# GNN message kernel: one sum along the parts' axis in place of four adds, and VectorE's work behind the table in another order

## The reference, cut to what matters

```python
h = jnp.maximum(_layernorm(x, axis=-1), 0.0)
x_i, x_j = h[dst], h[src]
tmp = jnp.concatenate([x_i, x_j, edge_attr], axis=1)
msg = jax.nn.relu(tmp @ W1 + b1) @ W2 + b2
x = x + jax.ops.segment_sum(msg, dst, num_segments=12500)
```

## Time and profile before

| | |
|---|---|
| time, median of 3 runs | 3531.99 us (3527.91 to 3535.4) |
| profiled execution: time | 3524.77 us |
| profiled execution: span of its instructions | 3522.9 us |
| PE busy | 3298.3 us (94%), 21992 matmuls |
| DVE busy | 2710.3 us (77%) |
| POOL busy | 2665.2 us (76%) |
| ACT busy | 1994.9 us (57%) |
| mean granted TensorE clock | 0.966 |

### The profile page before, as it was taken

The page is one execution under the profiler, slowest core; times in us unless marked ns, Lnnn a source line. Parts: engine busy times, 40 slices in busy tenths (PEclk is TensorE's granted clock), DMA queues, the critical chain, the costliest instruction groups (busy, mean ns, idle before and its releaser), DMA issues.

```text
span 3522.9 us, 96768 instructions
## 1 busy us (share of the span) xinstructions
PE 3298.3 (94%) x21992; PEld 2982.0 (85%) x21992; DVE 2710.3 (77%) x7030; ACT 1994.9 (57%) x7413; POOL 2665.2 (76%) x2768
## 2 busy tenths in 40 slices
PE   7699999999999999999999999999999999999998
PEld 6698888888888888888888888888888888888887
DVE  7787788887777777777777777777777777777774
ACT  6466666655555555555555555555555555555553
POOL 7677777777777777777777777777777777777776
PEclk9999999999999999999999999999999999999996
DMA  9543434333333333333333333333333333333434
GB/s 276 119 110 106 108 107 109 105 106 100 103 102 104 101 104 101 103 101 104 102 102 102 100 105 101 105 100 105 100 104 101 105 101 106 99 106 98 106 100 104
DMA packets 286659, 380.48 MB, mean 108 GB/s; under 512 B 90916, under 2 KB 190549, under 8 KB 285542
## 3 DMA queue, kind: packets, MB, share of 16 engines
q0 software_dynamic: 88064, 177.91, 20.4%
q1 hardware_dynamic: 198342, 201.58, 19.6%
q10 hardware_dynamic: 208, 0.49, 0.1%
HBM read 362.58 MB, written 17.04 MB: 108 GB/s over the span
## 4 chain that ended last, share of the span: by engine, by line
PE 31%; POOL 27%; issue 22%; DMA 8%; ACT 6%; DVE 4%; DVEq 1%; SPq 0%; POOLq 0%; ACTq 0%
POOL gath L540 26%; PE ps L1285 13%; DMA gath<-b_table,idx 7%; PE ps L1269 7%; PE ps L1261 6%; ACT work L675 2%; DVE gath L990 2%; PE ps L1308 2%; ACT gath L656 2%; PE ps L1237 1%; PE ps L1316 1%; PE ps L1295 1%; PE ps L1275 1%; ACT work L698 1%; ACT idx L640 0%
## 5 line engine op out<-in xcount | busy, mean ns | idle before, releaser
L540 POOL DMA_INDIRECT gath<-b_table,idx x2688 | 2588.8, 963 | 826.8 <-issue 757.6
L1285 PE MATMUL ps<-h_tab,p_hot 128*128 128x480 f32 (+1 forms) x6768 | 1588.3, 380 | 0.0
L1285 PEld LDWEIGHTS ps<-h_tab,p_hot 128*128 128x128 f32 x6768 | 1247.7, 195 | 80.9
L675 ACT ACTIVATE work<-ps,work 128x80 f32<-128x80 f32 x4136 | 977.8, 331 | 474.3 <-PE ps L1285 467.3
L656 ACT ACTIVATE gath<-gath 128x512 f32<-128x512 f32 (+1 forms) x768 | 443.6, 578 | 923.5 <-DVE gath L990 920.6
L1269 PEld LDWEIGHTS ps<-onehot,gath 128*128 128x128 f32 x5376 | 696.7, 196 | 262.1 <-ACT gath L656 246.5
L1269 PE MATMUL ps<-onehot,gath 128*128 128x48 f32 x5376 | 743.0, 279 | 167.5 <-ACT gath L656 163.6
L1261 PE MATMUL ps<-rhs,lhs 96*128 96x128 f32 x5376 | 804.9, 292 | 35.5 <-DVE lhs L981 35.5
L990 DVE TENSOR_TENSOR gath<-ps,gath 128x512 f32<-128x512 f32 (+1 forms) x768 | 479.6, 624 | 426.2 <-DMA gath<-b_table,idx 397.4
L1261 PEld LDWEIGHTS ps<-rhs,lhs 96*128 96x128 f32 x5376 | 694.4, 200 | 37.2 <-issue 35.7
L981 DVE TENSOR_SCALAR_CACHE_REDUCE lhs<-nodes 48x512 f32<-48x512 f32 (+1 forms) x768 | 520.0, 677 | 32.9 <-DMA rhs<-a_table 2.6
(11 more groups left out here) (128 smaller groups left out, 1887.0 us busy)
## 6 DMA issues: line engine op xcount, KB each, us to landing
nodes<-dst_row SPq DMA_DIRECT2D x494, 96.0 KB
gath<-b_table,idx POOLq DMA_INDIRECT x2688
nodes<-dst_row SPq DMA_DIRECT2D x384, 72.0 KB
lhs<-in_edge_t SPq DMA_DIRECT2D x384, 64.0 KB
work<-key_row SPq DMA_DIRECT2D x94, 256.0 KB
lhs<-in_edge_t SPq DMA_DIRECT2D x384, 48.0 KB
rhs<-a_table SPq DMA_DIRECT2D x768, 24.0 KB
work<-in_edge_t SPq DMA_DIRECT2D x220, 32.0 KB
```

The costliest lines, as they stand in the source:

```text
L540: pool.indirect_dma_start(gath[:, u, t, :], None, b_table, bass.IndirectOffsetOnAxis(ap=idx[:, u, t:t + 1], axis=0)).then_inc(gathered[u], 16)
L675: m = nc.scalar.activation(p_sel[:, t % 2, at_j, :], ps_run[:, q, j * words:(j + 1) * words], ACT.Copy, scale=p_mask[:, at_j, t:t + 1])
L1285: mm = nc.tensor.matmul(ps_run[:, q, 0:m * words].rearrange("p (j w) -> p j w", j=m), p_hot[:, t % 2, i, :], h_tab[:, first:first + BLOCKS ...
```

## The change

`sum_picked` added the 11 parts in four instructions, each waiting for the one before: 5 parts to 5 (400 elements in each partition), 3 to 3 (240), 1 to 1 (80) and 1 to 1 (80). Now it is one `tensor_reduce` that reads `p_sel` transposed, 80 words by 11 parts, and writes 80 words; its inner step is 80 words. This happens 376 times.

Behind the table DVE's order is new: packings stand between the early statistics, the one-hots of the first three steps come before `early_stats(4)` and the early writes, and ACT's copies of chunks 3 to 6 stand ahead of its wait for the statistics.

```diff
@@ -726,10 +726,10 @@
                     if j == 6 and not first:
                         rectify_tail(place_p(c - 1, it))
 
+            for c in range(3, chunks):
+                keep_words(c)
             act.wait_ge(early_var, len(early_parts))
             nc.scalar.activation(early_stat[:, 3, :], early_stat[:, 2, :], ACT.Sqrt).then_inc(early_std, 1)
-            for c in range(3, chunks):
-                keep_words(c)
             weigh_b2(0, 0)
             rectify(0, 0)
             act.wait_ge(early_ready, 2)
@@ -941,25 +941,17 @@
             split_lo(chunks - 1)
 
             find_rel()
-            for q in range(1, len(early_parts)):
-                early_stats(q)
-            pack_words(3)
-            dve.wait_ge(early_std, 1)
-            nc.vector.reciprocal(early_stat[:, 4, :], early_stat[:, 3, :]).then_inc(early_rstd, 1)
-            dve.wait_ge(early_rstd, 1)
-            dve.wait_ge(rel_ready, kinds)
-            for rows, first, count in ((early_b, 0, EARLY_B), (early_a, EARLY_B, EARLY_A), (early_c[:], EARLY_B + EARLY_A, EARLY_C)):
-                part = slice(first, first + count)
-                nc.vector.scalar_tensor_tensor(early_h[:, part, :], rows, 0.0,
-                                               early_stat[:, 4, part].unsqueeze(2).to_broadcast([P, count, feat]),
-                                               ALU.max, ALU.mult).then_inc(early_ready, 1)
-            for c in range(4, chunks):
-                pack_words(c)
-            dve.wait_ge(words_kept, chunks - 1)
-
-            dve.wait_ge(iota_copied, 2)
-            dve.wait_ge(first_ready, 1)
-            dve.wait_ge(ones_ready, 4)
+            def write_early():
+                dve.wait_ge(early_std, 1)
+                nc.vector.reciprocal(early_stat[:, 4, :], early_stat[:, 3, :]).then_inc(early_rstd, 1)
+                dve.wait_ge(early_rstd, 1)
+                dve.wait_ge(rel_ready, kinds)
+                for rows, first, count in ((early_b, 0, EARLY_B), (early_a, EARLY_B, EARLY_A),
+                                           (early_c[:], EARLY_B + EARLY_A, EARLY_C)):
+                    part = slice(first, first + count)
+                    nc.vector.scalar_tensor_tensor(early_h[:, part, :], rows, 0.0,
+                                                   early_stat[:, 4, part].unsqueeze(2).to_broadcast([P, count, feat]),
+                                                   ALU.max, ALU.mult).then_inc(early_ready, 1)
 
             def make_hot(k, it):
                 s, u, n = it * PERIOD + k, k % SLOTS, step_tiles(k)
@@ -1030,18 +1022,11 @@
 
             def sum_picked(t, c, it):
                 n = c + it
-                done = 3 * (n * TILES + t)
-                sel = p_sel[:, t % 2, :, :]
                 dve.wait_ge(p_picked, n * runs + 2 * (t + 1))
-                nc.vector.tensor_tensor(sel[:, 0:5, :], sel[:, 0:5, :], sel[:, 6:11, :], ALU.add).then_inc(p_sum_step, 1)
-                dve.wait_ge(p_sum_step, done + 1)
-                nc.vector.tensor_tensor(sel[:, 0:3, :], sel[:, 0:3, :], sel[:, 3:6, :], ALU.add).then_inc(p_sum_step, 1)
-                dve.wait_ge(p_sum_step, done + 2)
-                nc.vector.tensor_tensor(sel[:, 0, :], sel[:, 0, :], sel[:, 1, :], ALU.add).then_inc(p_sum_step, 1)
-                dve.wait_ge(p_sum_step, done + 3)
                 if t == 0 and c:
                     dve.wait_ge(p_unpacked, 2 * n)
-                nc.vector.tensor_tensor(p_words[:, t, :], sel[:, 0, :], sel[:, 2, :], ALU.add).then_inc(p_h_ready, 1)
+                nc.vector.tensor_reduce(p_words[:, t, :], p_sel[:, t % 2, :, :].rearrange("p j w -> p w j"), AX.X, ALU.add
+                                        ).then_inc(p_h_ready, 1)
 
             def unpack_words(c, it):
                 n = c + it
@@ -1149,11 +1134,26 @@
                     if final and j == 4:
                         set_flags()
 
-            for k in range(LEAD):
-                if k == 3:
-                    add_z(0, 0)
+            pack_words(3)
+            early_stats(1)
+            early_stats(2)
+            pack_words(4)
+            early_stats(3)
+            pack_words(5)
+            pack_words(6)
+            dve.wait_ge(words_kept, chunks - 1)
+            dve.wait_ge(iota_copied, 2)
+            dve.wait_ge(first_ready, 1)
+            dve.wait_ge(rel_ready, kinds)
+            dve.wait_ge(ones_ready, 4)
+            for k in range(LEAD - 1):
                 make_hot(k, 0)
                 make_hot_t(k, 0)
+            early_stats(4)
+            write_early()
+            add_z(0, 0)
+            make_hot(LEAD - 1, 0)
+            make_hot_t(LEAD - 1, 0)
             dve.wait_ge(words_kept, chunks)
             key_hot(0, 0, 0)
             cycle(0, 0, first=True)
```

More of the change, by code:

```diff
@@ L269, in gnn @@
         pack_step, packed, words_kept = sem("pack_step"), sem("packed"), sem("words_kept")
-        p_sum_step, ident_copied = sem("p_sum_step"), sem("ident_copied")
+        ident_copied = sem("ident_copied")
         unpack_step, p_unpacked = sem("unpack_step"), sem("p_unpacked")
```

## The result

The changed kernel takes 3473.37 us in the median (3468.78 to 3475.12, 4 runs), the one before 3529.95 us beside it (3526.54 to 3535.4): a ratio of 0.9836, 95% interval 0.9819 to 0.9853. Forecast were 3475. The two profiled executions stand 49.65 us apart (3524.77 and 3475.12), not the 56.6 of the medians, and the way the gain is made up differs from the forecast.

A forecast was written before the change was run, and what follows sets the result against it. The prediction took POOL's gather chain as the bound: 50.0 us from the adds' hold plus 7.1 from the hole, 57.1 off 3524.77, gave 3467.7; adding 7.2 for the median of the runs gave 3474.9 us, range 3464 to 3496.

The forecast's parts named there:

- POOL's gathers as the one chain: Whole run: POOL gathers without waiting for work, so shortening its chain shortens the kernel one for one until PE takes over.
- (1) The adds hold the gathers: From 131 us on: gathers starting during two-SBUF-input adds are held; removing the adds gains 50.0 us, bounds 40 and 51.
- (2) The reduce at 1070 ns: DVE's 880-element sum: 1070 ns at full speed against 1.54 us for the adds, worth nothing by itself.
- the bound that I had worked out, 3.5 us: DVE's sum in each step: only a reduce longer than 3.5 us would make DVE bound the cycle.
- (3) The hole closes wholly: Behind the table: POOL's 7.39 us idle gap at 122.66 us closes through DVE's new order, gaining 7.1 us, bounds 3 and 7.3.
- Landing is not waited for long: Behind the table, before the one-hots: `a_table` rows issued by 97.1 us cause no long wait; one-hots end at 101.8.
- Can PE keep up: Cycles at the new 34.9 us period: PE fits barely, 0.1 us free in cycles 2 to 16, 1.1 in mid-run.
- The sum: Whole kernel: 50.0 + 7.1 = 57.1 us gained, giving 3474.9 us, 1.6% less; chance 0.80.
- the reduce holds the gathers: Rival, chance 0.03: gathers starting inside DVE's reduce are held some 0.43 us, +82 us, 3614 us.
- Slow read: Rival, chance 0.03: the transposed read takes 4 ns an element, the reduce 3.7 us; DVE bounds, 3563 us.
- The lengthening stays: Rival, chance 0.05: the adds do not lengthen the gathers, other instructions do; only the hole closes, 3525 us.
- PE as bound: Rival, chance 0.09: PE holds cycles at 35.2 instead of 34.9 us, gain shrinks by 28 us, 3503 us.

The follow-up runs named there:

- the twins: Changed kernel plus, before each reduce, a 400-element add with two SBUF inputs or a 400-element reduce with one: ratios 0.9982 and 1.0138 on slow chips.
- the mark: The changed kernel, unaltered, run again on a usual chip beside other variants: 3468.82 us against 3525.41 for the kernel before, ratio 0.9842.
- the twin: Changed kernel plus a 400-element reduce with one SBUF input before each reduce: 4916.16 us on a slow chip, ratio 1.0138 to the kernel before.

## Why the prediction was right

*POOL's gathers as the one chain:* right on the usual chips, and not on the slow kind. The distance between the last gathers, 49.8 us, is that between the profiled executions, 49.65, and 235 us of DVE's work taken away changed nothing.

*(1) The adds hold the gathers, 50.0 us:* right, and shown by the exchange of the sum alone and by the twins. The gathers that start inside the adds are held for 49.9 us in all. Measured as gained are 48.0, 49.5 and 49.5 us in the changed kernel, the reduce alone and the changed kernel again (2588.8 less 2540.8, 2539.3 and 2539.3). One reading beside it was too narrow: of the six lengthened gathers behind the table, put down to two-input instructions, two (1.22 us at 108.98, 1.03 at 110.51) start inside packing instructions with one input, the first of them shown in the last section.

*(2) The reduce at 1070 ns:* the wrong term. It takes 1685 in the change. The failed step is the one in which I chose full speed for an inner step of 80 words "since it needs one element a step and no second stream"; read in order it takes 1059. The formula of the Trainium skill, VectorE: DVE Perf Modes, that also gave 1.07 us is stated there for `tensor_tensor`, and here it fits the reduce that reads in order alone. DVE is 80% busy, not 73%. It cost nothing, because the bound that I had worked out, 3.5 us, was far off; the decision to price what it takes to matter, not only the likeliest value, held the forecast.

*(3) The hole closes wholly, 7.1 us:* right in size on average (6.9 us from the order alone, 3525.41 to 3518.56; the gather behind the hole at 115.88), wrong in the profiled execution (1.6 us). "Landing is not waited for long" was said of `a_table` rows; the landing that I left out is that of gathered rows. The first `add_z` waits 2.19 us for it in the mark, and in the profiled execution, where SP came to its two loads of 672 KB a microsecond sooner, DVE waits 9.08 us for the last early rows. That the loads are what delays the rows agrees with all landings on record, but was not tested on its own.

*Can PE keep up:* it did in the changed kernel, barely. PE is busy 98 to 99% in cycles 3 to 15 (the first counted as 0), and POOL's only long waits are the two behind the table. Counted along the timelines, the median lead of the index copy fell from near 8 us to 5.8 in cycle 3 and 3.9 in cycle 16, and its least is 1.1 us, just behind them in cycle 17. In the profiled execution of the one reduce with the old order it ran out there, at a granted clock of 0.90 and with PE busy all the time (700 to 717 us); POOL (timeline):

```profile
706.83 0.94 POOL L540 DMA_INDIRECT gath<-b_table,idx  x1 [1.49 <-ACT idx L640]
...
715.96 0.94 POOL L540 DMA_INDIRECT gath<-b_table,idx  x1 [0.71 <-issue]
```

Less the usual 0.30 each, that is 1.6 us: PE does become the bound there for a moment.

*The sum:* 57.1 forecast, 56.6 between the medians, 49.65 between the profiled executions. The profiled execution before (3524.77) was faster than all four of its timed runs (3526.54 to 3535.4) and the one after (3475.12) the slowest of its four, so the good agreement of 3475 and 3473.37 is in part luck. The mark, beside the kernel before on chip 0, gained 56.6 us again.

*The rivals:* the reduce holds the gathers: excluded by the 593 gathers that start inside it and by the twin. Slow read: true by its mechanism at 1.9 ns an element (1685 / 880), under the 4 at which it would decide. The lengthening stays: excluded. PE as bound: no waits of POOL in the changed kernel, 1.6 us in one execution of the one reduce, so a matter of a microsecond or two and not of 28; and PE had the lower clock for less of the time than before, not more (mean 0.982 for 0.966).

The Trainium skill, SBUF — State Buffer, "Who interferes with whom", explains an earlier measurement, in which `tensor_tensor` did not stall a DMA, by the inference that it takes only the read interface. That does not carry over to this case: the gathers, which read their indices from SBUF, are held by it, 38.8 us by 376 instructions. Its line that `tensor_reduce` never contends on trn2 agrees with the twin's mean of 944 ns.

## What to carry to other kernels

Look for the engine that never waits, not for the one that is busiest: POOL was 76% busy and was the whole kernel. Lay its timeline beside the other engines' and ask what is running when one of its equal instructions comes out long; here an add with two SBUF inputs on another engine cost more by where it read than by how long it took. When work is moved earlier, check which transfers were issued behind it only by chance, and take the result on more than one chip before calling it a gain.

## What the runs showed of the hardware that was not expected

- A gather that starts while DVE works on two SBUF inputs is held to the end of that instruction less 0.12 to 0.13 us. Of the 198 gathers that start inside the 400-element adds of the kernel before 171 are lengthened, all but those that start in the first 0.04 or the last 0.14 us of the add. In the twins 400-element adds cost 38.8 us in 2688 gathers, a reduce of the same length nothing.
- Two inputs are not the only way to hold a gather. In the kernel before, L824 reads and writes one SBUF tensor, 672 int32 words in 0.50 us, and the gather that starts inside it takes 1.22 us, again to L824's end less 0.13. POOL and DVE (timelines):

```profile
108.98 1.22 POOL L540 DMA_INDIRECT gath<-b_table,idx  x1 [0.30 <-issue]
...
108.88 0.50 DVE L824 TENSOR_SCALAR work<-work 128x672 int32<-128x672 int32 x1
```

- A TENSOR_REDUCE of 880 fp32 elements takes 1685 ns with an inner step of 80 words and 1059 in order; ACT's copies of 80 words from PSUM take 332 ns written in order and 406 written 11 words apart.
- On the usual chips the 34 executions with the four adds whose clock is on record had a mean granted clock of 0.963 to 0.971, the 23 without them 0.980 to 0.988, though PE's busy share is the same (94% in both profiles). I have no experiment on the cause.
- The same kernel takes 3525 us on some chips and 4870 on others, and the change's own ratio goes from 0.984 to 1.02 between them.
